# Two batches normalised early by VectorE, the maxima's rows ahead of the values, and a batch's tail two chunks up in the slots

## What is computed

```python
x = x + tanh(g_xattn[0]) * L0_xattn(layernorm(x), ctx, ctx)    # 16 heads of 8, Wq bq Wk bk Wv bv Wo bo
x = x + tanh(g_ffn[0])   * L0_ffn(layernorm(x))                # SwiGLU, inputs and weights rounded to fp4 in blocks of 16
x = x + tanh(g_xattn[1]) * L1_xattn(layernorm(x), ctx, ctx)    # additive mask, relu(ctx @ Wo.T + b)
x = x + tanh(g_ffn[1])   * L1_ffn(layernorm(x))                # expert 0 of 8, relu, an inner layer norm
x = x + tanh(g_xattn[2]) * L2_xattn(layernorm(x), ctx, ctx)    # 8x8 weights in each head, mask by where
x = x + tanh(g_ffn[2])   * L2_ffn(layernorm(x))                # one linear layer in fp8, scales by abs-max
x = x + tanh(g_xattn[3]) * L3_xattn(layernorm(x), ctx, ctx)    # mask per batch
x = x + tanh(g_ffn[3])   * L3_ffn(layernorm(x))                # 16 experts, top 4 of 2 groups of 4, and a shared one

def fp4_quant_dequant(x):                                      # of x and of the weights in L0_ffn
    xb = x.reshape(shape[:-1] + (shape[-1] // 16, 16))
    scale = maximum(max(abs(xb), -1) / 6.0, 1e-12)
    q = GRID[searchsorted(MID, abs(xb / scale))] * sign(xb) * scale
```

## Time and profile before

| | before |
|---|---|
| median of 3 runs | 872.09 us (871.35 to 875.77) |
| the profiled execution itself | 875.11 us, its span 873.3 us |
| PE busy | 649.6 us, 74% of the span |
| VectorE busy | 554.5 us, 64% |
| ACT busy | 300.6 us, 34% |
| GpSimd busy | 279.4 us, 32% |
| chain that ended last, by engine | PE 39%, VectorE 27%, GpSimd 11%, issue 11%, DMA 5% |

### The profile page before, as it was taken

How to read it: one execution, slowest core, us unless ns; L and a number is a source line. 1 busy time by engine, 2 the same in 40 slices (tenths; PEclk the granted TensorE clock), 3 DMA queues, 4 the chain that set the end, 5 groups by cost and what they waited for, 6 DMA issues and landing times.

```text
span 873.3 us, 9977 instructions
## 1 busy us (share of the span) xinstructions
PE 649.6 (74%) x2926; PEld 402.0 (46%) x2926; DVE 554.5 (64%) x1432; ACT 300.6 (34%) x559; POOL 279.4 (32%) x580
## 2 busy tenths in 40 slices
PE   5577754666447999988389896136878979889997
PEld 3333322444326666456144342013334557667775
DVE  7666566988824444547755555684465887888754
ACT  3034231222221343533104343010445545545554
POOL 6101221114431212216414152151022245544554
PEclk9559677688757999979659998555698999999999
DMA  9755221000022342200514532003250123243432
GB/s 267 146 160 157 37 68 28 0 1 1 1 65 66 88 120 48 83 8 1 160 22 118 157 61 57 0 24 99 79 146 3 47 69 105 86 135 86 134 108 61
DMA packets 67989, 67.71 MB, mean 78 GB/s; under 512 B 25119, under 2 KB 48223, under 8 KB 67552
## 3 DMA queue, kind: packets, MB, share of 16 engines
q1 hardware_dynamic: 61406, 64.64, 26.9%
q10 hardware_dynamic: 6530, 2.44, 1.1%
HBM read 50.29 MB, written 17.60 MB: 78 GB/s over the span
## 4 chain that ended last, share of the span: by engine, by line
PE 39%; DVE 27%; POOL 11%; issue 11%; DMA 5%; ACT 3%; SPq 1%; ACTq 1%; POOLq 0%; DVEq 0%
POOL sg L623 7%; PE ps L1503 7%; PE ps L1455 6%; PE ps L1483 5%; DVE mraw L1104 4%; DVE st L939 3%; DVE xn L965 3%; PE ps L1436 2%; PE ps L1419 2%; DMA QG<-q_parts 2%; PE ps L1605 1%; PE ps L1407 1%; PE ps L1487 1%; PE ps L1486 1%; DVE mv L942 1%
## 5 line engine op out<-in xcount | busy, mean ns | idle before, releaser
L1104 DVE TENSOR_REDUCE mraw<-ps 128x4 f32<-128x308 f32 x256 | 115.8, 476 | 93.5 <-PE ps L1455 35.9
L707 ACT ACTIVATE PT<-ps 110x512 f32<-110x512 f32 x192 | 111.7, 596 | 175.7 <-PE ps L1483 87.0
L1455 PE MATMUL ps<-KG,QG 98*128 98x308 f32 x256 | 111.8, 475 | 46.0 <-DVE mraw L1104 31.2
L623 POOL TENSOR_TENSOR sg<-sg,cb 128x512 f32<-128x512 f32 x64 | 84.5, 1323 | 74.2 <-ACT sg L832 71.2
L1483 PE MATMUL ps<-QG,KG 128*110 128x512 f32 x192 | 97.4, 523 | 12.4 <-DMA QG<-mT 7.2
L1455 PEld LDWEIGHTS ps<-KG,QG 98*128 98x128 f32 x256 | 60.7, 242 | 95.8 <-DVE mraw L1104 66.7
L541 POOL TENSOR_TENSOR nt<-nhv,rs 128x4 f32<-128x4 f32 (+1 forms) x99 | 25.1, 254 | 210.0 <-DVE rs L946 204.8
L1503 PE MATMUL ps<-PT,VN 128*18 128x512 f32 x512 | 75.6, 666 | 0.0
L1311 DVE TENSOR_TENSOR ps<-ps,sg 128x512 f32<-128x512 f32 x72 | 50.3, 698 | 39.6 <-POOL sg L623 36.6
L484 POOL CAST mhl<-mraw 128x64 fp32r<-128x64 f32 x16 | 4.8, 301 | 188.4 <-DVE mraw L1104 177.3
L1483 PEld LDWEIGHTS ps<-QG,KG 128*110 128x110 f32 x192 | 36.5, 195 | 54.2 <-ACT PT L707 31.1
(11 more groups left out here) (275 smaller groups left out, 1440.7 us busy)
## 6 DMA issues: line engine op xcount, KB each, us to landing
cb<-c_parts SPq DMA_DIRECT2D x64, 256.0 KB, 3.3
QG<-q_parts SPq DMA_DIRECT2D x48, 256.0 KB, 4.0
KG<-k_parts SPq DMA_DIRECT2D x48, 154.0 KB, 3.0
q_parts<-hiT SPq DMA_DIRECT2D x14, 256.0 KB, 2.0
q_parts<-loT SPq DMA_DIRECT2D x14, 256.0 KB, 2.0
k_parts<-kmH SPq DMA_DIRECT2D x16, 154.0 KB, 2.2
k_parts<-kmL SPq DMA_DIRECT2D x16, 154.0 KB, 2.4
VN<-v_parts SPq DMA_DIRECT2D x16, 144.0 KB, 2.7
```

Source lines behind the costliest of these rows:

```text
L623: pool.tensor_tensor(sg[:, n % 3, :], sg[:, n % 3, :], cb[:, k % CRING, :], ALU.mult).then_inc(sc_done, 1)
L707: act.activation(PT[0:w, q % PTR, :], ps[0:w, 4 + q % 2, :], ACT.Exp, scale=SCALE[l]).then_inc(exp_done, 1)
L1104: dve.tensor_reduce(mraw[:, n % 2, i, g * HG:(g + 1) * HG], ps[:, u % 2, 0:GK].rearrange("p (h k) -> p h k", k=K), AX_X, ALU.max).then_inc ...
L1455: ins = pe.matmul(o, QG[0:KS, n % 3, g, q], KG[0:KS, n % 3, g, :], start=True, stop=l not in (1, 2))
```

## The change

In the beginning, in layer 0:

- `refine_first` does batches 0 and 1 on VectorE; GpSimd refines batches 2 and 3 in one go (before: 1, 2 and 3). VectorE applies the norm to batch 1 right behind `loT` of batch 0, and takes the statistics of batches 2 and 3 only after it.
- GpSimd builds `l2w` (the weights of layer 2's keys) between the key rows of layers 0 and 1. PE and ACT have the keys and values of layer 3 behind the queries of batch 1.
- SP issues one of the three transfers of key constants ahead of layer 1's keys and the two others behind the queries of batch 0; the queries of batch 1 go ahead of the weights of `ffn0`. The transfers of the first `mT` are split: head groups 0 and 1 on SP, now ahead of the first two `values_in`, groups 2 and 3 on ACT right behind the copy that makes `mT`.

In all slots: `turn_sums` of the second half moves from chunk 3 to 2, `normalise` of it from 5 to 3, `att_transposed` from 6 to 4, `attT_out` from 7 to 5, `project` from 8 to 6, the residual from 9 to 7, and the application of the next norm to batch k-2 from 9 to 6. The halves of `quantise_input` move from chunks 10 and 11 to 6 and 8, around the residual. The weights of layer 0 are rounded in slot 0 (chunks 6 and 8) and slot 1 (chunk 8), none in slot -1; `quantise_weight8` moves from chunk 10 to 8. What is computed stays the same, and the number of instructions changes by that of one `refine_first` against one batch less in `refine`'s.

```diff
--- before
+++ after
@@ -224,7 +224,7 @@
         ld_x = [sem(f"ld_x{b}") for b in range(B)]
-        ld_neg, neg_in, ld_rows = sem("ld_neg"), sem("neg_in"), sem("ld_rows")
+        ld_neg, neg_first, neg_in, ld_rows = sem("ld_neg"), sem("neg_first"), sem("neg_in"), sem("ld_rows")
         v_fill, v_out = [sem(f"v_fill{l}") for l in range(L)], [sem(f"v_out{l}") for l in range(L)]
@@ -300,6 +300,11 @@
+        def maxima_in(eng, n, groups):
+            eng.wait_ge(mT_ready, n + 1)
+            for g in groups:
+                eng.dma_start(QG[98:106, n % 3, g, :].bitcast(F32), mT[32 * g:32 * g + 32, n % 2, :].bitcast(F32)).then_inc(mg_in[n % 3], 16)
+
         def values_out(eng, l):
@@ -362,11 +367,6 @@
-            def maxima_in(n):
-                sp.wait_ge(mT_ready, n + 1)
-                for g in range(G):
-                    sp.dma_start(QG[98:106, n % 3, g, :].bitcast(F32), mT[32 * g:32 * g + 32, n % 2, :].bitcast(F32)).then_inc(mg_in[n % 3], 16)
-
             def store(b):
@@ -384,19 +384,23 @@
             next_mask(0)
+            def key_constants(r, done):
+                sp.dma_start(KG[96:P, r, :, :].rearrange("p g k -> p (g k)").bitcast(F32), kst).then_inc(done, 16)
+
             keys_out(0)
+            sp.wait_ge(ld_neg, 16)
+            key_constants(0, neg_first)
             keys_out(1)
-            sp.wait_ge(ld_neg, 16)
-            for r in range(3):
-                sp.dma_start(KG[96:P, r, :, :].rearrange("p g k -> p (g k)").bitcast(F32), kst).then_inc(neg_in, 16)
             keys_in(0)
             queries_in(0)
+            key_constants(1, neg_in)
+            key_constants(2, neg_in)
             keys_in(1)
+            queries_in(1)
             ffn0_weights()
-            queries_in(1)
+            maxima_in(sp, 0, (0, 1))
             values_in(0)
             values_in(1)
-            maxima_in(0)
             keys_out(2)
@@ -418,7 +422,7 @@
                     if 0 <= k + 1 < B and l * B + k + 1 > 0:
-                        maxima_in(l * B + k + 1)
+                        maxima_in(sp, l * B + k + 1, range(G))
                     if l == 2 and k == 1:
@@ -529,7 +533,7 @@
-            ln_count = [1]
+            ln_count = [2]
@@ -555,14 +559,14 @@
             key_rows(0)
-            key_rows(1)
             for w in range(3):
...
             last.then_inc(l2w_ready, 1)
-            refine(1, 3)
+            key_rows(1)
+            refine(2, 2)
             pool.wait_ge(ld_ident, 16)
@@ -715,10 +719,10 @@
                     kv_out(2)
-                    kv_out(3)
                 xT_one(1)
                 if l == 0:
+                    kv_out(3)
                     parts_out(1)
@@ -731,7 +735,9 @@
                             maxima_out(k + 1)
-                        if c == 7 and 1 <= k <= last:
+                            if l == 0 and k == -1:
+                                maxima_in(act, 0, (2, 3))
+                        if c == 5 and 1 <= k <= last:
                             attT_out(l * B + k - 1)
@@ -946,10 +952,10 @@
-            def refine_first():
-
-                v, t, y = nhv[:, 0:TPB], nt[:, 0:TPB], rs[:, 0:TPB]
-                dve.wait_ge(stats_ready, 1)
+            def refine_first(b):
+
+                v, t, y = [w[:, b * TPB:(b + 1) * TPB] for w in (nhv, nt, rs)]
+                dve.wait_ge(stats_ready, b + 1)
                 for step in range(3):
@@ -1126,7 +1132,7 @@
                 def after(k, c):
-                    if c == 9 and k - 2 >= 0 and l < 3:
+                    if c == 6 and k - 2 >= 0 and l < 3:
                         normalise_batch(2 * l + 1, k - 2)
@@ -1141,15 +1147,15 @@
                             input_low(1)
-                    if c in (10, 11) and l == 0 and k - 2 >= 0:
-                        quantise_input(k - 2, c - 10)
+                    if c in (6, 8) and l == 0 and k - 2 >= 0:
+                        quantise_input(k - 2, (c - 6) // 2)
                     if c == 9 and k == 0:
...
                         normalise_batch(2 * l, 2)
-                    if c == 10 and l == 0 and k in (-1, 0, 1):
-                        quantise_weight(k + 1)
-                    if c == 10 and l == 2 and k == 1:
+                    if l == 0 and (k, c) in ((0, 6), (0, 8), (1, 8)):
+                        quantise_weight(2 * k + (c == 8) - (k == 1))
+                    if c == 8 and l == 2 and k == 1:
                         quantise_weight8()
@@ -1159,14 +1165,16 @@
                 if l == 0:
-                    dve.wait_ge(ld_x[3], 16)
-                    statistics(x, 3)
+                    normalise_batch(0, 1)
+                    keys_and_values(1)
+                    for b in (2, 3):
+                        dve.wait_ge(ld_x[b], 16)
+                        statistics(x, b)
                     bias_values()
...
                     keys_and_values(3)
-                    normalise_batch(0, 1)
                     dve.wait_ge(v_evac, L)
@@ -1180,12 +1188,12 @@
                             q_rest(k + 2)
-                        if c == 5 and k >= 1:
+                        if c == 3 and k >= 1:
                             normalise(l * B + k - 1, 1)
-                        if c == 9 and k >= 1 and l < 3:
+                        if c == 7 and k >= 1 and l < 3:
                             residual_read(k - 1)
                             residual(k - 1)
-                        if c == 9 and k >= 1 and l == 3:
+                        if c == 7 and k >= 1 and l == 3:
                             last_residual(k - 1)
@@ -1335,15 +1343,13 @@
             statistics(x, 0)
-            refine_first()
+            refine_first(0)
             normalise_batch(0, 0)
...
             statistics(x, 1)
-            keys_and_values(1)
-            dve.wait_ge(ld_x[2], 16)
-            statistics(x, 2)
+            refine_first(1)
             for l in range(L):
@@ -1443,6 +1449,8 @@
                         pe.wait_ge(kg_in[n % 3], 48 * uses(n))
+                        if n == 1:
+                            pe.wait_ge(neg_in, 32)
                         if l == 1:
@@ -1514,12 +1522,12 @@
                     pe.wait_ge(ld_w2, 16)
-                    keys_and_values(3)
                 turn_input(1)
                 if l == 0:
+                    keys_and_values(3)
                     pe.wait_ge(k_lo, L)
-                    pe.wait_ge(neg_in, 48)
+                    pe.wait_ge(neg_first, 16)
                     pe.wait_ge(ones_set, 1)
@@ -1538,13 +1546,13 @@
                             weighted_sums(k, c // 11, c // 7 % 2 * (c < 11))
-                        if c == 3 and k >= 1:
+                        if c == 2 and k >= 1:
                             turn_sums(l * B + k - 1, 1)
-                        if c == 6 and k >= 1:
+                        if c == 4 and k >= 1:
                             att_transposed(l * B + k - 1)
                             turn_maxima(k + 1)
-                        if c == 8 and k >= 1:
+                        if c == 6 and k >= 1:
                             project(l * B + k - 1)
```

## The result

The changed kernel takes 865.88 us (median of 6 runs, 863.41 to 869.45) where the kernel before takes 874.70 (6 runs, 871.35 to 881.05): a ratio of 0.990, 95% interval 0.9872 to 0.9928. Timed again it took 867.40 (8 runs) against 875.67, 0.9911 (0.9877 to 0.9945). The forecast was 848.8 with a range of 839 to 860. It was faster, as forecast, by 8 to 9 us instead of 23. (The forecast started from 872.09, the median of three runs; the six runs here have 874.70, so 2.6 us of the distance in the absolute time are the base's.)

What follows compares the result with a forecast made beforehand. TensorE, the busiest engine, was taken to stand still for VectorE in layer 0. Terms -4.3, -1.2, -14, -2.3 and -1.5 sum to -23.3: 851.8 from the profiled 875.11, 848.8 for the median (from 872.09), range 839 to 860.

Steps and rivals of the forecast that it cites:

- beginning and slot 0: Layer 0's start to batch 3 turned: earlier first maximum and maxima's rows, less a second rounding; -4.3 us (-1.5 to -7).
- slot 1's end: Layer 0: TensorE's wait of 5.58 us ahead of slot 2 shrinks by 1.2 us (bounds 0, -3).
- slots 2 to 4: Layer 0: fp4 rounding fills VectorE's waits, so the first product of `ffn0` comes 14 us earlier (bounds -6, -17).
- layer 2: Shorter wait before slot 2 and gains in the last tail, less 0.6 on GpSimd's mask work: -2.3 us (+1, -4).
- layer 3 and experts: Batch 3's tail comes a little earlier and the experts with it, their part unchanged: -1.5 us (0, -3).
- PE waits 2.4 for `xn`: End of layer 0's slot 0: two roundings and `xn` on VectorE end at 61.9, TensorE being ready at 59.5.
- a chance of 0.15 and 3.7 us: Rival: the new 2.4 us wait lowers TensorE's clock in slot 1, +3.7 us, so 852.5; chance 0.15.
- a stretch of equal work takes longer at a lower granted clock: Sign, for any stretch of the kernel, that would show the forecast wrong; no size given.
- rival D: Follow-up experiments' rival: layer 3's loss is the clock's accident, so its edits stay within 1 to 1.5 us; no chance given.
- rival "half": Slots 2 and 3: the tail's read isn't two chunks earlier, -6 us in all for that term, 856.8; chance 0.14.
- the one on the other side: Slots with a tail and next batch, layers 0 to 3: maxima's rows come later, slower by 4 to 12, 878; chance 0.02.
- rival "clock up": Shorter waits keep TensorE's clock up in slot 2 or 3: 845.1, in both 841.4; chance 0.17.

Runs made afterwards that it cites:

- the old tail in layer 3: Layer 3's tail back at its old chunks: in the changed kernel 864.45 us (0.9877), in a version with weights replaced and five loads late 859.77 (0.9826).

## Why the prediction was wrong

The sum by its own steps, in the profiled execution:

| step | forecast | measured | from |
|---|---|---|---|
| beginning and slot 0 | -4.3 | -3.6 | batch 3 turned, 66.26 and 62.65 |
| slot 1's end | -1.2 | -2.0 | the wait, 5.58 and 3.60 |
| slot 1's clock | 0 | +7.0 | the windows, 19.22 and 26.23 |
| slots 2 to 4 | -14 | -15.6 | first product, from slot 2's start |
| layers 0's and 1's feed-forward, layer 1 | 0 | +0.3 | -14.2 to -13.9 |
| layer 2 | -2.3 | -0.7 | -13.9 to -14.6 |
| layer 3 and experts | -1.5 | +3.9 | -14.6 to -10.7 |
| sum | -23.3 | -10.7 | |

Of the 12.6 us between the sums 7.0 are slot 1's clock and 5.4 layer 3 with the experts; the other rows together make 0.2.

**The failed step is the one that ended slot 0**: "PE waits 2.4 for `xn`". The wait was counted as its 2.4 us and slot 1's clock as unchanged. What the wait does to the 19 us behind it stood among the rivals, with a chance of 0.15 and 3.7 us, and the last of the prediction's own signs, "a stretch of equal work takes longer at a lower granted clock", is what came. In slot 1 it is worth 7: 7.0 in the changed kernel's trace, 7.0 where the same was added to the kernel before (26.17, 19.22), 6.6 back where the wait was filled. In the whole kernel's time it is worth 7.2 by taking the weight away from slot 0 and 7.3 by adding the same to the kernel before (by the medians 6.4 and 5.6), and 3.3, not resolved, by filling the wait. The price was too low because it was taken from slot 2 of the kernel before (21.84 at 0.64 against some 18), where the clock had come back for the last part, and for a slot with other work; slot 1's own busy time at either level, 15.8 and 23.6, was the row to use. The chance was too low because "2.4 is less than half of it", of 5.58, was taken for a reason. The runs show no such proportion: slot 1 was slow behind waits of 2.06, 2.53, 2.92, 3.02, 3.23 and 3.95 us and at 1.00 behind 1.12 and in seven of the ten profiles with no wait there (0.85 to 0.93 in the three others). The Trainium skill, "TensorE: Matmul & The Clock Gate", section "What's actually happening", knows the two levels, 1.2 and 2.4 GHz, with the lower one behind idleness. The traces agree (0.62 in slot 1 behind the wait of 3.02, 1.00 where it was filled to 1.12), and the prediction's sentence beside it ("a new one may hurt slot 1") named the right slot.

**The second failed step is layer 3.** The tail was taken to come "a little earlier and with it the experts". It gave back 3.9. In its slots the queues were not looked through: in the last one VectorE has the router of batch 0 between, the tail's normalisation stands behind it, and TensorE waits for it. In the timeline of the changed kernel, and at the same place of the kernel before, where a shorter wait for `xn` stood:

```profile
663.50 1.12 PE L1419 MATMUL ps<-ident,att 128*128 128x128 f32 x4 [3.29 <-DVE att L1003]
```

```profile
676.70 1.08 PE L1385 MATMUL ps<-ident,xn 128*128 128x128 f32 x4 [1.90 <-DVE xn L965]
```

That is 1.4 us more, and taking the 3.29 away brought little. The larger part is lost behind the attention, in the experts' first batch. Two of its `sg` on ACT, at 709.07 and 729.83 in the kernel before, at 696.06 and 719.15 in the changed one, lie 20.8 us apart in all five profiles with the old tail in layer 3, and 21.5 to 24.4 in all twelve with the new one: here 2.3 of the 3.9 go, and the clock's accident (rival D) would not sort the profiles so. The four microseconds from the second product that waits over 1 us for `hL` show the clock, before and after:

```profile
709.18:713.18 4.00, 3.91 (x18) 2.93 (x19) 3.93 (x5) 1.64 (x3) 2.60 (x2) 1.00 0.49 147
```

```profile
696.18:700.18 4.00, 4.00 (x11) 3.17 (x12) 3.93 (x5) 1.43 (x3) 1.67 (x1) 0.59 0.51 151
```

Why the clock is low there after the new tail stays open. The waits for `hL` just ahead are 2.60 and 1.86 us against 2.60 and 1.59 before, and in a profile with the old tail 2.59 and 1.98, with the clock at 1.00 behind them.

**What was right.** The landing of the maxima's rows, the filled waits of VectorE in slots 2 and 3 (the largest term), the bound of the first product by TensorE and ACT, and that `mT` is late nowhere by much: the waits for `QG<-mT` add up to 5.7 us against 7.2 before, though one of 1.18 in slot 2 is new. (The prediction took from the earlier trace rows that there is none beyond the first. Those rows end at 270 us; the trace before has one at each layer's first product, 2.53, 2.21, 0.94 and 1.48.) The rival "half" is refuted by 15.6; the one on the other side too, and it didn't follow from its own terms: 2.0 us in eight places are 16, less than the 23 to be eaten.

**What was luck.** The 15.6 has some of the rival "clock up" in it. In slot 2 of the changed kernel the clock came back soon, and TensorE asked for `att` 21.0 us after the slot's start (115.88 - 2.45 - 92.48), where the forecast had kept before's 24.8. From slot 2's start to the first product of `ffn0` it is 56.1 us in six of the fourteen profiles with the new chunks and 57.6 to 59.1 in the other eight, the changed kernel's second profile (58.8) among them; the forecast's 57.2 lies between. And the beginning's -4.3 was right for a bundle only: the earlier start is worth 6.5 at slot 0's first product (47.26, 40.75), of which the second rounding took 3 at its end. With the rounding left in slot -1, 3.0 of the 6.5 go to the weights' late loads (43.79), a queue that the prediction passed over.

## What to carry to other kernels

A wait that a change adds is not paid by its length alone: look at what TensorE does after it, and price that stretch at both clock levels by its own busy time. When an engine's queue is refilled to cover a wait, ask for each item which transfer feeds it and whether its old place was free because something else was late. And a wait of about 2 us may be there in some executions only, as with the queries here: one profile of a variant doesn't tell its median, and it helps to know which of its runs was profiled.

## What the runs showed of the hardware

- A wait of 2 to 4 us of TensorE was followed by slot 1 at a lower clock in all six profiles that had it: 24.7 to 26.3 us in five and 28.5, its own 2.06 included, in the sixth, against 19.2 to 19.7 at full clock without a further wait. Repeating transposes whose result was already there, 20 of them, made the slot 6.6 us shorter and the kernel, by ratios whose intervals overlap, 3.3 us faster.
- The clock comes back at very different speed, behind the same wait and in the same kernel. After the 3.60 ahead of slot 2 the changed kernel had 0.57 for four microseconds and then 1.00; in its second profile, after 3.61, it had 0.50 for sixteen (90.92 to 106.92). In the kernel before it was 0.50 until about 106. I know no row that tells when.
- A write of 256 KB lands 2.0 us after its issue in the median. Issued right behind five bulk loads it was read back 5.8 and 6.0 us later (50.01 to 55.77; 49.74 to 55.73 in the changed kernel), and with these loads behind it 2.0 us later (50.97 to 52.99).
